# A one-core cross-attention and feed-forward kernel: the four compute engines' loops over tiles written out with fixed addresses

## The reference

```
h   = layernorm(x)
q   = (h @ Wq) * s;  k = (context @ Wk) * s;  v = context @ Wv      # s = 128 ** -0.25
x   = x + softmax(q k^T) v @ Wo + bo
n   = layernorm(x)
out = x + relu(n @ Ws1)**2 @ Ws2 + routed(n)
# routed: weights of the top 2 of 8 experts, softmaxed, then trunc()
```

## Time and profile before

| what | value |
|---|---|
| median of 3 runs | 116.21 us (116.04 to 116.53) |
| profiled execution's own time | 116.54 us |
| its span, first to last instruction | 114.7 us |
| PE busy | 109.2 us, 95% |
| DVE, ACT, POOL busy | 87.6, 85.9, 65.5 us |
| chain that ended last | PE 76%, DVE 7%, ACT 6%, DMA 4%, SP's queue 2%, issue 2% |
| loaded before the loops | by about 27 us nearly all inputs are in; later DMA is stores |

### The profile page before, as it was taken

The page is one execution under the profiler, slowest core; times in us unless marked ns, Lnnn a source line. Parts: engine busy times, 40 slices in busy tenths (PEclk is TensorE's granted clock), DMA queues, the critical chain, the costliest instruction groups (busy, mean ns, idle before and its releaser), DMA issues.

```text
span 114.7 us, 3118 instructions
## 1 busy us (share of the span) xinstructions
PE 109.2 (95%) x854; PEld 105.8 (92%) x854; DVE 87.6 (76%) x349; ACT 85.9 (75%) x349; POOL 65.5 (57%) x106
## 2 busy tenths in 40 slices
PE   6987999999999989999999999999999999999991
PEld 6975999899998989999999999999999999989980
DVE  1019888569889697797979797987979786979973
ACT  4006926997948979898988889898989888997330
POOL 2005735956372965785676578657856766259341
PEclk9999999999999999999999999999999999999998
DMA  2899999995000200031005000400400050013034
GB/s 55 256 334 364 357 352 352 348 348 184 1 6 0 91 0 3 6 130 53 0 0 183 0 0 24 159 0 0 150 33 0 0 183 3 0 61 122 0 137 137
DMA packets 11815, 12.70 MB, mean 111 GB/s; under 512 B 1056, under 2 KB 10272, under 8 KB 11808
## 3 DMA queue, kind: packets, MB, share of 16 engines
q1 hardware_dynamic: 11520, 12.36, 32.4%
q10 hardware_dynamic: 288, 0.26, 0.7%
HBM read 8.42 MB, written 2.10 MB: 92 GB/s over the span
## 4 chain that ended last, share of the span: by engine, by line
PE 76%; DVE 7%; ACT 6%; DMA 4%; SPq 2%; issue 2%; POOL 1%; ACTq 0%; DVEq 0%
PE o_ps L432 8%; PE o_ps L434 7%; PE o_ps L433 7%; PE s_ps L432 7%; PE s_ps L434 7%; PE s_ps L433 7%; PE g_ps L492 6%; DMA wqt_sb<-in_wq_t 4%; PE f_ps L522 4%; ACT probs L710 4%; PE g_ps L505 3%; PE f_ps L432 2%; PE g_ps L446 2%; PE s_ps L622 1%; DVE wq_mean L1079 1%
## 5 line engine op out<-in xcount | busy, mean ns | idle before, releaser
L710 ACT ACTIVATE probs<-s_ps,neg_max,rstd 128x77 f32<-128x77 f32 x112 | 45.4, 428 | 4.0 <-DVE neg_max L950 4.0
L840 POOL TENSOR_TENSOR probs<-probs,recip 128x308 f32<-128x308 f32 x27 | 19.0, 703 | 23.5 <-DVE recip L956 23.4
L710 ACT ACTIVATION_READ_ACCUMULATOR probs<-s_ps,neg_max,rstd 128x1 f32 x112 | 24.2, 216 | 0.0
L432 PE MATMUL o_ps<-u_hi,pt_hi 128*128 128x256 f32 (+1 forms) x80 | 22.7, 284 | 0.2 <-DVE pt_lo L961 0.2
L434 PE MATMUL o_ps<-u_lo,pt_hi 128*128 128x256 f32 (+1 forms) x80 | 22.4, 280 | 0.0
L433 PE MATMUL o_ps<-u_hi,pt_lo 128*128 128x256 f32 (+1 forms) x80 | 22.4, 280 | 0.0
L432 PE MATMUL s_ps<-a_hi,xt_hi 128*128 128x308 f32 x64 | 22.1, 345 | 0.0
L434 PE MATMUL s_ps<-a_lo,xt_hi 128*128 128x308 f32 x64 | 19.4, 303 | 0.0
L433 PE MATMUL s_ps<-a_hi,xt_lo 128*128 128x308 f32 x64 | 19.4, 303 | 0.0
L432 PEld LDWEIGHTS o_ps<-u_hi,pt_hi 128*128 128x128 f32 (+1 forms) x80 | 15.0, 188 | 0.6 <-DVE pt_lo L961 0.6
L433 PEld LDWEIGHTS o_ps<-u_hi,pt_lo 128*128 128x128 f32 (+1 forms) x80 | 15.1, 188 | 0.0
(11 more groups left out here) (190 smaller groups left out, 270.8 us busy)
## 6 DMA issues: line engine op xcount, KB each, us to landing
xt_sb<-in_x_t SPq DMA_DIRECT2D x8, 256.0 KB, 6.7
x_sb<-in_x SPq DMA_DIRECT2D x8, 256.0 KB, 6.7
x_sb<-x_tr SPq DMA_DIRECT2D x7, 256.0 KB, 2.3
out<-y_sb SPq DMA_DIRECT2D x6, 256.0 KB, 2.3
wqt_sb<-in_wq_t SPq DMA_DIRECT2D x4, 256.0 KB, 5.0
wo_sb<-in_wo SPq DMA_DIRECT2D x1, 1024.0 KB, 9.0
wk_sb<-in_wk_p SPq DMA_DIRECT2D x3, 256.0 KB, 3.1
wv_sb<-in_wv_p SPq DMA_DIRECT2D x2, 384.0 KB, 6.2
```

The costliest lines, as they stand in the source:

```text
L432: pe.matmul(out_ap, hi, rhs_hi, start=first, stop=False)
L710: e = act.activation(probs_of(t)[:, par, h * TK:(h + 1) * TK], s_ps[:, 2 * par + half, (h - half * H // 2) * TK:(h - half * H // 2 + 1) * TK],
L840: pool.tensor_tensor(rows, rows, recip[:, par, hs].unsqueeze(2).broadcast_to([P, H // 2, TK]), ALU.mult).then_inc(probs_ready, 1)
```

## The change

Three loops over tiles become Python loops, so that every t is a plain number: the helper `pairs` becomes `tiles_of`, and the loops of POOL and DVE are written with `range`. No instruction that computes is added, removed or moved; register instructions and loop branches of the four compute engines go, and each engine's program becomes longer by the written-out iterations (five more on PE, ACT and POOL, four more on DVE). SP's loop and the routed part's loops stay.

```diff
-        def pairs(eng, first, last, step):
-
-            with eng.Fori(first // 2, last // 2) as j:
-                for par in range(2):
-                    step(2 * j + par, par)
+        def tiles_of(first, last, step):
+
+            for t in range(first, last):
+                step(t, t % 2)
...
-            pairs(pe, 2, TILES - 2, step)
+            tiles_of(2, TILES - 2, step)
...
-            pairs(act, 2, TILES - 2, step)
+            tiles_of(2, TILES - 2, step)
...
-            with pool.Fori(1, TILES // 2 - 1) as j:
+            for j in range(1, TILES // 2 - 1):
                 step(2 * j, 0)
                 rstd_x(j + 1)
                 step(2 * j + 1, 1)
...
-            with dve.Fori(1, (TILES - TG) // 2) as j:
+            for j in range(1, (TILES - TG) // 2):
                 dve.wait_ge(rstd1_done, j + TG)
                 for par in range(2):
                     step(2 * j + par, par, TG)
```

## The result

The changed kernel takes 116.85 us (median; 116.56 at its fastest) against 116.44 us for the kernel before on the same chip, 0.41 us more; the ratio on record is 1.0039, with a 95% interval of 1.0024 to 1.0054. Two of its twenty runs, of 123.91 and 155.56 us at a granted clock of TensorE of 0.86 and 0.67 where all others have 0.99 to 1.00, are left out of the ratio. It is slower by 0.4%. That is under the 0.5% that the prediction called "about what cannot be told", but with eighteen runs against twenty it can be told. The forecast was 116.0.

A forecast was written before the change was run, and what follows sets the result against it. PE, busy nearly throughout, was taken as the bound. Copies -0.08 and tail -0.08 made -0.16 us, from a median of 116.21 to 116.05, rounded to 116.0; range 115.4 to 116.8.

The forecast's parts named there:

- DVE's registers on the way to `ffn_rows`: Loop steps, DVE's remainders before `ffn_rows`: no register time in the chain, 0; at t = 3 alone 0.03 us might return.
- ACT's copies: Loop steps: exponentials start about 0.09 us sooner, so late copies to `pt_hi` come on time; gain 0.08 us, 0.1 at most.
- the end: PE's branch past the routed part: its landing distance changes with the layout; put at 0, with 0.14 us either way.
- The tail: From 97 us on, tiles 14 and 15: ACT's exponential starts sooner, gaining 0.08 us; bounds 0 and 0.12.
- Branches and registers of PE: PE's loop: five taken branches of 0.21 us and the register instructions lie under cover of the running array; price 0.
- the first rival: Whole kernel: nothing comes back, the 0.16 us turn into longer waits for PE and each other; 116.2 us, chance 0.2.
- The entry: Loops' entry, t = 2: PE's wait comes from ACT's exponentials in t = 1, ahead of all loops, and stays; price 0.
- Longer programs: Instruction fetch for the written-out code: packets arrive ahead of need; price 0, up to 1.35 us if one came late.
- 6 or 7: Sign expected in the changed kernel's trace: queue q8, which had 3 packets, shows 6 or 7.
- the small form of the fourth: Late fetches of written-out code, here only at the last branch or the loop's end: 116.8 us; whole rival's chance 0.12.
- The third rival: PE's loop branches cost after all: 5 x 0.21 = 1.05 us come back, 115.1 us with the tail; chance 0.06.

The follow-up runs named there:

- the padding: 40 small memsets of an unused tile near the head of DVE's program; kernel after with them 1.0012, kernel before with them 1.0045.
- the padded kernel before: The kernel before, loops kept, with 40 small memsets of an unused tile added on DVE; ratio 1.0045 (1.0018 to 1.0072).

## Why the prediction was wrong

Two terms that were put at 0 failed, of about the same size: DVE's registers on the way to `ffn_rows` (+0.22 us, 0.08 up to t = 2 and 0.14 in the steps, net of the 0.05 that ACT's copies gave) and the end (+0.21). The tail gave 0.02 of its 0.08.

The step of the reasoning that failed is the one on DVE's registers on the way to `ffn_rows`: "L971 starts 0.03 us after the copy's end. So nothing on DVE in this chain is register time". The reading is right for the loop, but what it was read for is not: it asked what the register instruction costs, not what it carries. It carried a wait, and without it the wait needed another place. The written-out step t = 12 was in the trace before: there, L971 starts 0.10 us behind the copy, an EVENT_SEMAPHORE ahead of it (shown above, at 91.8). ACT and DVE at t = 12 of the kernel before:

```profile
91.16 0.60 ACT L696 ACTIVATE pt_hi<-g_ps 128x512 fp32r<-128x512 f32 x1
...
91.86 0.69 DVE L971 TENSOR_TENSOR pt_lo<-g_ps,pt_hi 128x512 fp32r<-128x512 f32 x1
```

The copy ends at 91.76. I used t = 12 for PE's distances only the earlier trace rows, where the missing L914 hides this.

The other steps, in the prediction's order:

- Branches and registers of PE at 0: right. The kernel with all but DVE written out has steps of 5.23, as before.
- ACT's copies, -0.08 us: the mechanism is right (the copy starts 0.64 us after the first transpose in both steps above, from 64.51 and 69.74), the size nearly: 0.05 us in the steps of the kernel with all but DVE written out, which has no short attention where the kernel before has one, so up to 0.11. In the kernel after it is used up by the late remainders.
- The tail, -0.08: wrong, 0.02. The exponential does start sooner, 0.04 us behind the negation. But PE's transposes of tile 14's probabilities were as late as ACT. PE and ACT in the kernel before (first two lines) and in the kernel after:

```profile
100.85 0.38 PE L492 MATMUL g_ps<-ident,probs 128*128 128x128 f32 x2
...
101.27 0.38 ACT L681 ACTIVATE pt_hi<-g_ps 128x256 fp32r<-128x256 f32 x1
...
101.12 0.38 PE L491 MATMUL g_ps<-ident,probs 128*128 128x128 f32 x2
...
101.33 0.21 ACT L709 ACTIVATION_READ_ACCUMULATOR probs<-s_ps,neg_max,rstd 128x1 f32 x1
101.54 0.38 ACT L680 ACTIVATE pt_hi<-g_ps 128x256 fp32r<-128x256 f32 x1
```

The copy follows PE's first transpose by 0.42 us in both. ACT's 0.08 us turned into idle time: an ACT instruction that waits for nothing starts 0.09 to 0.10 us after the start of the accumulator's reading ahead of it (neighbouring records overlap), and the copy starts 0.21 us after it, 0.13 before (101.14 to 101.27). The two bounds of the prediction, 0 and 0.12, both came from ACT's rows; PE's rows, which stood level with them, were left aside. It is what the first rival said, "nothing comes back at all".
- The entry at 0: wrong by 0.08. The first remainder of t = 2 met three more waits, for `x_in[2]`, `x_in[3]` and `rstd1_done`, and starts 0.13 us behind its copy. With the waits moved the term is gone (9.77).
- Longer programs at 0: right for the steps. q8 has the 7 packets that "6 or 7" allowed, and the steps of the kernel with all but DVE written out are not longer than those of before.
- The end at 0 with 0.14 either way: wrong by more than the bound, and on the wrong engine. PE's branch gave 0.11 and its drain 0.06 back; DVE's drain took 0.38; +0.21 in sum. I weighed PE's landing alone, because it was the last one before.

Of the rivals, the small form of the fourth, "a late landing of the last branch", gave 116.8 and came nearest. Half of it is right: DVE's late drain is such a landing by all that the padding shows (that it is an instruction fetch is not shown). The other half is a mechanism that no rival had. The third rival's rule from the Trainium skill (Runtime: NRT & Kernel Launch, Instruction fetch mechanics), that a taken branch breaks the fetching ahead, is limited there to a branch "whose target isn't in the current 2-page window". In the kernel before, q8 carries no packet between 46.3 and 115.0 us, so PE's loop called for no new block, by that rule no stall was due, and the prediction's "The trace does not agree" says more than this case can test. On DVE the loop's return took from 0.14 to 0.27 us with the place of the code, and that was on the path in the padded kernel before; that it is a fetch is not shown.

## What to carry to other kernels

When a loop is written out, look at what its register instructions carried: where two waits stand ahead of an instruction, ask for the one that ends last first, so that the instruction itself holds it, and check it in the trace by the distance from the releaser's end (0.03 or 0.10 us here). A gain on one engine is worth what the next engine in line leaves of it, so ask at each copy and each tail which two engines are level. Differences of 0.3 to 0.4% between two programs can come from the place of their code: the same padding made one kernel here faster and the other slower, so try each at more than one place before one is called better.

## What the hardware showed unexpectedly

- A wait in an EVENT_SEMAPHORE of its own on DVE costs 0.07 us after its release over one held by the computing instruction (0.102 against 0.032 us from the copy's end); at t = 2, with four waits ahead of the remainder, 0.13.
- DVE's last drain comes 0.15 to 0.16 us or 0.53 to 0.54 us behind its branch, nothing between, by the place of the code: early in six of the kernels above and in the kernel before, late in the others.
- PE's branch past the routed part takes 0.35 us where PE is looped and 0.24 where it is written out, the same in all kernels of each kind; whether the loop or the place of the code decides is not shown, since no kernel has PE's code moved otherwise.
- The starts of PE's fifteen attention matmuls span 1.65 to 1.66 us in most steps and 1.60 in some, at a granted clock of 1.00 in both; what decides is open.
